# A four-layer graph network on one core: POOL starts a pair of indirect transfers when the even transfer two back has landed, instead of when the pair two back has, and each buffer has two semaphores, by the transfer's parity

## The chip, the core and the metric

The kernel runs on one core of one Trainium2 chip. The metric is the device time of one execution in microseconds (us), median of several runs. The engines are named as in the profile: PE (TensorE), DVE (VectorE), ACT (ScalarE), POOL (GpSimd), SP (SyncE).

## The reference, cut to what matters

A graph of 3125 nodes of 64 features and 103125 directed edges goes through four blocks; each block's output is added to x and x is normalised.

```python
edge_index = jnp.stack([src, dst])
x = _layernorm(x + _L0_gnn_ref(x, edge_index, ...))                 # 4 message layers
x = _layernorm(x + _L1_gnn_ref(x, edge_attr_64, edge_attr_9, ...))  # attention over edges
x = _layernorm(x + _L2_gnn_ref(x, edge_index, edge_attr_16, ...))   # one message layer
x = _layernorm(x + _L3_gnn_ref(x, edge_index))                      # normalised sum of neighbours
```

A message layer computes, for every edge, two dense layers with silu on the rows of its two end nodes, and sums the results per node:

```python
m = jnp.concatenate([hc[row], hc[col]], axis=1)
m = jax.nn.silu(m @ w1 + b1)
m = jax.nn.silu(m @ w2 + b2)
agg = jax.ops.segment_sum(m, row, num_segments=N) * C
```

## The kernel before

The kernel first sorts the edges by an end node (once by source, once by destination) into tiles of 128 edges, so that all edges of a tile have one of their ends in one block of 128 nodes. There are 832 tiles. The end in that block is fetched by a product with a one-hot matrix on PE. The other end can be any node, so its row is fetched from memory by an indirect transfer: one transfer, issued by POOL, brings one row for each of 128 partitions.

Five stages issue such transfers, all of them on POOL's one queue:

- The first scatter (line 917, function `scatter_s_pool`): 806 transfers of 8 bytes a row, to the sorted order by source. It runs beside the sorting by destination.
- The second scatter (line 935, `scatter_d_pool`): 806 transfers of 1136 bytes a row. A turn is four of them (EW = 4). PE and ACT compute the rows, ACT's copy `eo` (line 1082) ends them.
- The message layers (line 1193, `messages_pool` in `edge_messages`): four layers of block 0 and the one of block 2, 104 turns each, eight gathers a turn (W = 8) of 256 bytes a row, into one of four buffers `gx`. The gather of turn i waits for the copied indices `gi` (DVE, line 1278) and for a free buffer; DVE reads the rows three turns later, in the sum `pre_s` (line 1313).
- The logits of block 1 (line 1820, `logits_pool`): 208 turns, four gathers a turn (GT = 4) of 1280 bytes a row. The gather of turn i waits for the indices (DVE, line 1929) and for `gx_read`, with which DVE (line 1909) gives free the buffer of four turns back, right behind its product `kv` (line 1906). PE transposes the rows (line 1857) one turn later, after the first half of the turn's main products (line 1832) and before their second half. Its main products are of edges that are two turns older still.
- The last stage, block 3 (line 2415, `conv_pool`): 104 turns, eight gathers a turn of 256 bytes a row; PE multiplies them (line 2430) three turns later, DVE adds (line 2456).

Every stage runs as a software pipeline: `turns` unrolls the body four times (AHEAD = 4) inside a loop on each engine, and the engines meet only at semaphores. What matters here is how POOL throttles its own queue. Transfers go in pairs (PAIR = 2). Each pair has a semaphore, four of them a buffer in the message layers and the last stage (`rows_in[j][0..3]`), two in the logits and in the second scatter. Before the first transfer of a pair POOL waits until both transfers of the pair two back have landed. So when a pair starts, the pair just before it may still be under way. A landing adds 16 to the semaphore. An instruction that waits on POOL holds all that is behind it on POOL; POOL has nothing but these transfers in these stages.

The readers of a buffer (DVE line 1310, PE lines 1853 and 2425, DVE line 1928, ACT and DVE in `rows_gone`) wait for all its semaphores.

## Time and profile before

| what | value |
|---|---|
| median of 3 runs | 14786.38 us (14730.6 to 14797.07) |
| the profiled execution | 14804.43 us, its span on the core 14802.3 us |
| PE busy | 8646.8 us, 58% of the span |
| POOL busy | 7760.8 us, 52% |
| DVE busy | 5955.3 us, 40% |
| ACT busy | 2260.6 us, 15% |
| granted TensorE clock, mean | 0.77 |

The shares are means over stages that differ much, so that they bound nothing by themselves. The stages stand one behind another, and the time is the sum of their lengths; the first scatter alone runs beside other work.

### The profile page before, as it was taken

How to read it: one execution, taken by the hardware profiler on the slowest of the kernel's cores; microseconds unless marked ns; L12 is line 12 of the kernel's file. 1: busy time of each engine (PE TensorE's matmuls, PEld its weight loads, DVE VectorE, ACT ScalarE, POOL GpSimd, SP SyncE). 2: the span in 40 equal slices, each digit the busy share in tenths (PEclk: the TensorE clock that was granted, in tenths of full speed). 3: DMA queues.
4: the chain of work that ended last, by engine and by line, in shares of the span. 5: the costliest groups of instructions: out<-in, count | busy, mean ns of one | idle time of the engine just before them, and what ended most of it. 6: DMA issues, size and time to landing. Idle time of an engine off the chain costs nothing. (4 is left out here: it accounts for less than half of the span.)

```text
span 14802.3 us, 187298 instructions
## 1 busy us (share of the span) xinstructions
PE 8646.8 (58%) x45093; PEld 7115.8 (48%) x45094; DVE 5955.3 (40%) x14867; ACT 2260.6 (15%) x3991; POOL 7760.8 (52%) x7547
## 2 busy tenths in 40 slices
PE   2004778775555565555555555899994556664333
PEld 1004654444445455445444544788884545554232
DVE  5105730002333233333333333688888833333222
ACT  0000013330000100010001000355551000000000
POOL 5662025665555566546564656355552455554666
PEclk9999987876677666766676767899997867676555
DMA  1001333332111211121111111588884311111111
GB/s 24 1 1 61 108 121 119 117 111 54 38 38 36 62 39 39 37 60 39 38 39 48 39 37 39 169 250 251 251 251 110 103 42 41 41 41 29 22 22 22
DMA packets 853401, 1107.27 MB, mean 75 GB/s; under 512 B 336739, under 2 KB 530568, under 8 KB 852294
## 3 DMA queue, kind: packets, MB, share of 16 engines
q1 hardware_dynamic: 304698, 470.90, 10.9%
q0 software_dynamic: 264160, 418.34, 10.5%
q10 hardware_dynamic: 284332, 215.58, 5.6%
q8 instruction: 88, 1.44, 0.0%
q14 instruction: 123, 1.01, 0.0%
HBM read 896.28 MB, written 207.86 MB: 75 GB/s over the span
## 5 line engine op out<-in xcount | busy, mean ns | idle before, releaser
L1193 POOL DMA_INDIRECT gx_l<-xr,gi_l x4160 | 4231.1, 1017 | 3370.6 <-DVE gi_l L1278 2061.9
L1300 DVE TENSOR_TENSOR aggT_l<-aggT_l,psum 64x128 f32 x4160 | 1160.2, 279 | 3868.5 <-remote 1816.0
L1832 PE MATMUL psum<-cw,xa 128*128 128x256 f32 x6656 | 1519.2, 382 | 28.6 <-issue 21.3
L935 POOL DMA_INDIRECT slots_d<-eo,row_d x806 | 786.0, 975 | 1341.0 <-DVE eo L949 852.7
L1820 POOL DMA_INDIRECT gx<-xr,gi x832 | 896.0, 1077 | 1011.9 <-DVEq L1909 634.6
L1832 PEld LDWEIGHTS psum<-cw,xa 128*128 128x128 f32 x6656 | 1233.5, 190 | 252.9 <-issue 101.2
L1356 PE MATMUL psum<-ptab,oht 128*128 x6656 | 1017.9, 304 | 565.8 <-issue 506.4
L1356 PEld LDWEIGHTS psum<-ptab,oht 128*128 128x128 f32 x6656 | 953.8, 221 | 634.7 <-issue 633.7
L1232 PE MATMUL psum<-b,onesb 3*128 3x512 bf16 x520 | 260.7, 501 | 1650.6 <-ACT h_l L1259 1124.9
L2415 POOL DMA_INDIRECT gx_l<-xr,gi_l x832 | 834.6, 1003 | 473.9 <-DVE gi_l L2440 224.2
L1889 ACT COPY xT<-psum 32x512 f32<-32x512 f32 x1664 | 957.4, 575 | 611.8 <-remote 397.4
L917 POOL DMA_INDIRECT slots_s<-rec_s,row_s x806 | 801.7, 995 | 431.8 <-issue 418.5
L1234 PE MATMUL psum<-w,h_l 128*128 128x128 f32 x4160 | 879.4, 377 | 0.0
L1232 PEld LDWEIGHTS psum<-b,onesb 3*128 3x128 bf16 x520 | 49.5, 95 | 1720.1 <-issue 1691.8
L1234 PEld LDWEIGHTS psum<-w,h_l 128*128 128x128 f32 x4160 | 748.7, 270 | 181.3 <-issue 181.3
L1271 ACT ACTIVATE msg_l<-psum 128x512 f32<-128x512 f32 x520 | 310.6, 597 | 3315.7 <-remote 1843.7
L1259 ACT ACTIVATE h_l<-psum 128x512 f32<-128x512 f32 x520 | 310.6, 597 | 3296.6 <-remote 2372.8
L1245 PE MATMUL psum<-oh,msg_l 128*64 128x128 f32 x4160 | 733.6, 345 | 78.9 <-issue 78.4
L1313 DVE TENSOR_TENSOR pre_s_l<-psum,gx_l 128x512 f32<-128x512 f32 x520 | 359.7, 692 | 1008.3 <-remote 591.6
L1245 PEld LDWEIGHTS psum<-oh,msg_l 128*64 128x64 f32 x4160 | 644.1, 181 | 144.2 <-issue 132.5
L1245 PE MATMUL psum<-oh_b_l,msg_l 128*64 128x128 f32 x4160 | 678.2, 329 | 35.7 <-issue 30.1
L585 PE MATMUL psum<-oh_hi,oh_lo 128*128 128x25 bf16 x808 | 37.7, 183 | 1042.3 <-DVE oh_lo L522 692.0
(361 smaller groups left out, 13292.9 us busy)
## 6 DMA issues: line engine op xcount, KB each, us to landing
wkv<-slots_d ACTq DMA_DIRECT2D x208, 568.0 KB
kr<-keyrow_s SPq DMA_DIRECT2D x416, 256.0 KB
shb<-shT SPq DMA_DIRECT2D x1664, 64.0 KB
gx_l<-xr,gi_l POOLq DMA_INDIRECT x4992
vtab<-kv ACTq DMA_DIRECT2D x208, 256.0 KB
v_in<-vtab SPq DMA_DIRECT2D x104, 512.0 KB, 3.4
hT<-noderow SPq DMA_DIRECT2D x101, 512.0 KB
kr<-keyrow_d SPq DMA_DIRECT2D x208, 128.0 KB
```

Source lines behind the costliest of these rows:

```text
L917: scattered[j].at(pool.indirect_dma_start(slots["s"], bass.IndirectOffsetOnAxis(ap=row["s"][:, c:c + 1], axis=0), rec_s[:, c, :], None, bo ...
L935: e_gone[j][t // PAIR].at(pool.indirect_dma_start(slots["d"], bass.IndirectOffsetOnAxis(ap=row["d"][:, c0 + t:c0 + t + 1], axis=0), eo[j][ ...
L1193: pool.indirect_dma_start(gx[j][:, c_, :], None, xr, bass.IndirectOffsetOnAxis(ap=gi[j][:, c_:c_ + 1], axis=0)).then_inc(rows_in[j][h].sem ...
L1234: ins = pe.matmul(bank[2][:, q * P:(q + 1) * P], h1[:, q * P:(q + 1) * P], w2[:], start=False, stop=True, skip_group_check=True)
L1245: ins = pe.matmul(sums(j, t // per), msg[j][:, t * D:(t + 1) * D], ohs[j][:, t, :], start=t % per == 0, stop=(t + 1) % per == 0)
L1300: ins = dve.tensor_tensor(a, a, sums(j, h), ALU.add)
L1313: dve.tensor_tensor(pre_s[j][:], bank[0][:, :], gx[r][:, :, :].rearrange("p t f -> p (t f)"), ALU.add).then_inc(pre_done.sem, 1)
L1356: ins = pe.matmul(bank[0][:, t * D:(t + 1) * D], oht[:, t * P:(t + 1) * P], ptab[:, bass.ds(bl[t // PER["s"]] * D, D)], start=True, stop=True)
L1820: pool.indirect_dma_start(gx2[r][:, t, :], None, xr2, bass.IndirectOffsetOnAxis(ap=gi1[j][:, t:t + 1], axis=0)).then_inc(rows_in1[r][h].se ...
L1832: ins = pe.matmul(bank[2 + p][:, t % 2 * OKV:(t % 2 + 1) * OKV], xa[j][:, c, t * P:(t + 1) * P], cw[:, c, :], start=c == 0, stop=c == KC - 1)
L1889: ins = act.copy(xT2[j][q * DQ:(q + 1) * DQ, h, :], bank[0][h * DQ:(h + 1) * DQ, :])
L2415: pool.indirect_dma_start(gx[j][:, c_, :], None, xr, bass.IndirectOffsetOnAxis(ap=gi[j][:, c_:c_ + 1], axis=0)).then_inc(rows_in3[j][h].se ...
```

## The change

Transfers are no longer told apart by pairs but by parity (TURNS = 2). Each buffer, and each scatter, has two semaphores: one for its even transfers and one for its odd ones. POOL waits only ahead of an even transfer, until the even one two back has landed. The odd transfer behind it starts without a wait. Whether the odd transfer two or three back has landed is not asked. The number of waits on POOL is the same, one for two transfers; the readers of a buffer wait for two semaphores where they waited for four (logits and second scatter: two before and after). Nothing that is computed or moved changes.

```diff
-PAIR = 2
+TURNS = 2
...
             for c in range(EC):
-                j = c // PAIR % 3
+                j = c % TURNS
...
-                if c >= 2 * PAIR and c % PAIR == 0:
-                    two_back = scattered[(c // PAIR - 2) % 3]
-                    pool.wait_ge(two_back.sem, two_back.n)
+                if c >= TURNS and c % TURNS == 0:
+                    pool.wait_ge(scattered[j].sem, scattered[j].n)
...
                 for t in range(i * EW - c0, EW):
-                    if i and t % PAIR == 0:
-                        two_back = e_gone[(i - 1) % AHEAD][t // PAIR]
+                    if (i or t >= TURNS) and t % TURNS == 0:
+                        two_back = e_gone[j if t >= TURNS else (i - 1) % AHEAD][t % TURNS]
...
                         for c_ in range(W):
-                            h = c_ // PAIR
-                            if c_ % PAIR == 0 and (h >= 2 or k.has(0, 1)):
-                                s_, two_back = (0, rows_in[j][h - 2]) if h >= 2 else (1, rows_in[k.buf(1, AHEAD)][h + 2])
-                                pool.wait_ge(two_back.sem, two_back.n + k.uses(s_, AHEAD) * (16 * PAIR))
+                            h = c_ % TURNS
+                            if c_ >= TURNS and h == 0:
+                                pool.wait_ge(rows_in[j][h].sem, rows_in[j][h].n + (k.uses(0, AHEAD) - 1) * (16 * W // TURNS) + 16 * (c_ // TURNS))
+                                pool.nop(nofuse=True)
+                            elif c_ < TURNS and k.has(0, 1) and h == 0:
+                                of = rows_in[k.buf(1, AHEAD)][h]
+                                pool.wait_ge(of.sem, of.n + k.uses(1, AHEAD) * (16 * W // TURNS))
                                 pool.nop(nofuse=True)
...
                     for t in range(GT):
-                        h = t // PAIR
-                        if t % PAIR == 0 and k.has(0, 1):
-                            two_back = rows_in1[k.buf(1, AHEAD)][h]
-                            pool.wait_ge(two_back.sem, two_back.n + k.uses(1, AHEAD) * (16 * PAIR))
+                        h = t % TURNS
+                        if t >= TURNS and h == 0:
+                            pool.wait_ge(rows_in1[r][h].sem, rows_in1[r][h].n + (k.uses(0, AHEAD) - 1) * (16 * GT // TURNS) + 16 * (t // TURNS))
+                            pool.nop(nofuse=True)
+                        elif t < TURNS and k.has(0, 1) and h == 0:
+                            of = rows_in1[k.buf(1, AHEAD)][h]
+                            pool.wait_ge(of.sem, of.n + k.uses(1, AHEAD) * (16 * GT // TURNS))
                             pool.nop(nofuse=True)
```

The last stage has the same edit as the message layers, and the readers' loops over `range(W // PAIR)` become loops over `range(TURNS)`.

On POOL, one turn inside the loop of the first message layer stands like this before. The names in brackets are the semaphores that a row waits for; `s_rows_in1_2` is buffer 1, pair 2.

```order
L1183 REGISTER_ALU
L1185 REGISTER_ALU [waits s_gi_set]
L1193 DMA gx2_l0<-xr,gi2_l0 128x64 [waits s_pre_done,s_rows_in1_2]
L1193 DMA gx2_l0<-xr,gi2_l0 128x64
L1193 DMA gx2_l0<-xr,gi2_l0 128x64 [waits s_rows_in1_3]
L1193 DMA gx2_l0<-xr,gi2_l0 128x64
L1193 DMA gx2_l0<-xr,gi2_l0 128x64 [waits s_rows_in2_0]
L1193 DMA gx2_l0<-xr,gi2_l0 128x64
L1193 DMA gx2_l0<-xr,gi2_l0 128x64 [waits s_rows_in2_1]
L1193 DMA gx2_l0<-xr,gi2_l0 128x64
```

After the change the same turn is:

```order
L1182 REGISTER_ALU
L1184 REGISTER_ALU [waits s_gi_set]
L1195 DMA gx2_l0<-xr,gi2_l0 128x64 [waits s_pre_done,s_rows_in1_0]
L1195 DMA gx2_l0<-xr,gi2_l0 128x64
L1195 DMA gx2_l0<-xr,gi2_l0 128x64 [waits s_rows_in2_0]
L1195 DMA gx2_l0<-xr,gi2_l0 128x64
L1195 DMA gx2_l0<-xr,gi2_l0 128x64 [waits s_rows_in2_0]
L1195 DMA gx2_l0<-xr,gi2_l0 128x64
L1195 DMA gx2_l0<-xr,gi2_l0 128x64 [waits s_rows_in2_0]
L1195 DMA gx2_l0<-xr,gi2_l0 128x64
```

The transfers stand in the same order. The third row waits for the pair 4 and 5 of the turn before and becomes a wait for transfer 6 of that turn, and the later ones wait for transfers 0, 2 and 4 of the same turn.

On POOL, one turn of the logits loop before:

```order
L1788 REGISTER_ALU
L1788 REGISTER_ALU [waits s_gi1_set]
L1820 DMA gx22<-xr2,gi10 128x320 [waits s_turned1,s_gx_read,s_rows_in1_0]
L1820 DMA gx22<-xr2,gi10 128x320
L1820 DMA gx22<-xr2,gi10 128x320 [waits s_rows_in1_1]
L1820 DMA gx22<-xr2,gi10 128x320
```

And after:

```order
L1790 REGISTER_ALU
L1790 REGISTER_ALU [waits s_gi1_set]
L1825 DMA gx22<-xr2,gi10 128x320 [waits s_turned1,s_gx_read,s_rows_in1_0]
L1825 DMA gx22<-xr2,gi10 128x320
L1825 DMA gx22<-xr2,gi10 128x320 [waits s_rows_in2_0]
L1825 DMA gx22<-xr2,gi10 128x320
```

The wait ahead of the third transfer was for the second pair of the turn before (`s_rows_in1_1`); it is now for the first transfer of the same turn (`s_rows_in2_0`).

## Rows read from the trace of the kernel before

**Rows 1.** The view by windows: busy us (x instructions) of each engine, granted TensorE clock, DMA share, GB/s.

```profile
81.00:1235.00 1154.00, 102.69 (x811) 58.08 (x811) 220.78 (x281) 0.00 (x0) 801.43 (x806) 1.00 0.04 6
...
2066.00:3362.00 1296.00, 1021.44 (x3197) 530.16 (x3195) 59.82 (x247) 433.17 (x598) 785.73 (x806) 0.79 0.35 116
...
4858.00:6272.00 1414.00, 800.74 (x4539) 686.25 (x4537) 473.90 (x1179) 127.95 (x216) 840.35 (x832) 0.69 0.19 45
...
9389.00:11171.00 1782.00, 1739.42 (x9031) 1505.84 (x9032) 1531.64 (x3076) 995.99 (x1858) 896.04 (x832) 0.99 0.84 250
...
11882.00:13461.00 1579.00, 964.40 (x5494) 853.05 (x5494) 475.72 (x1187) 147.36 (x301) 852.64 (x831) 0.70 0.18 41
...
13546.00:14771.00 1225.00, 374.01 (x1642) 357.84 (x1642) 311.62 (x1016) 0.00 (x0) 834.58 (x832) 0.50 0.12 22
```

**Rows 2.** The page's costliest groups: indirect transfers that POOL issues, in four stages.

```profile
L1193 POOL DMA_INDIRECT gx_l<-xr,gi_l x4160 | 4231.1, 1017 | 3370.6 <-DVE gi_l L1278 2061.9
...
L935 POOL DMA_INDIRECT slots_d<-eo,row_d x806 | 786.0, 975 | 1341.0 <-DVE eo L949 852.7
...
L1820 POOL DMA_INDIRECT gx<-xr,gi x832 | 896.0, 1077 | 1011.9 <-DVEq L1909 634.6
...
L2415 POOL DMA_INDIRECT gx_l<-xr,gi_l x832 | 834.6, 1003 | 473.9 <-DVE gi_l L2440 224.2
```

**Rows 3.** POOL in order of time, layer stage: start us, us, in brackets idle before and releaser.

```profile
3383.55 0.94 POOL L1193 DMA_INDIRECT gx_l<-xr,gi_l  x1 [0.30 <-issue]
...
3386.05 0.94 POOL L1193 DMA_INDIRECT gx_l<-xr,gi_l  x1 [0.31 <-DMA gx_l<-xr,gi_l]
```

**Rows 4.** POOL in order of time, layer stage, two turns and the next start.

```profile
6023.57 1.72 POOL L1193 DMA_INDIRECT gx_l<-xr,gi_l  x1 [9.22 <-DVE gi_l L1278]
...
6043.34 0.94 POOL L1193 DMA_INDIRECT gx_l<-xr,gi_l  x1 [0.30 <-issue]
...
6049.67 1.72 POOL L1193 DMA_INDIRECT gx_l<-xr,gi_l  x1 [5.38 <-DVE gi_l L1278]
```

**Rows 5.** All engines in order of time, logits stage, one turn.

```profile
10005.91 0.94 POOL L1820 DMA_INDIRECT gx<-xr,gi  x1 [3.46 <-DVEq L1909]
...
10005.92 0.34 ACTq L1877 DMA_DIRECT2D wkv<-slots_d  x1
...
10007.50 0.60 PE L1857 MATMUL psum<-ident,gx 128*64 128x128 f32 x4
...
10010.00 1.30 POOL L1820 DMA_INDIRECT gx<-xr,gi  x1 [0.30 <-issue]
...
10012.82 0.69 DVE L1906 TENSOR_TENSOR kv<-gx,wkv 128x512 f32<-128x512 f32 x1
...
10014.46 0.94 POOL L1820 DMA_INDIRECT gx<-xr,gi  x1 [3.16 <-DVEq L1909]
```

**Rows 6.** POOL in order of time, logits stage, where a transfer ended the wait.

```profile
10024.30 0.95 POOL L1820 DMA_INDIRECT gx<-xr,gi  x1 [0.30 <-issue]
...
10031.81 0.94 POOL L1820 DMA_INDIRECT gx<-xr,gi  x1 [3.49 <-DMA gx<-xr,gi]
```

**Rows 7.** POOL in order of time, last stage, four turns.

```profile
13968.50 1.14 POOL L2415 DMA_INDIRECT gx_l<-xr,gi_l  x1 [4.42 <-DVE gi_l L2440]
...
14009.79 0.94 POOL L2415 DMA_INDIRECT gx_l<-xr,gi_l  x1 [0.30 <-issue]
...
14015.87 1.13 POOL L2415 DMA_INDIRECT gx_l<-xr,gi_l  x1 [5.13 <-DVE gi_l L2440]
```

**Rows 8.** POOL in order of time, second scatter.

```profile
2513.69 0.97 POOL L935 DMA_INDIRECT slots_d<-eo,row_d  x1 [0.30 <-issue]
...
2516.29 1.01 POOL L935 DMA_INDIRECT slots_d<-eo,row_d  x1 [0.30 <-DMA slots_d<-eo,row_d]
```

**Rows 9.** Waits of DVE over the run: us in total, times, longest.

```profile
DVE aggT_l L1300 <- issue: 1348.0, 1461, 18.7
```

**Rows 10.** DVE in order of time, last stage.

```profile
14109.98 0.22 DVE L2456 TENSOR_TENSOR conv<-conv,psum 128x64 f32 x1 [3.25 <-issue]
```

More of the change, by code:

```diff
@@ L891, in first_column @@
             return min(i * EW, EC - EW)
-        scattered = [sig(f"scattered{j}") for j in range(3)]
+        scattered = [sig(f"scattered{j}") for j in range(TURNS)]
         feats_in = [sig(f"feats_in{j}") for j in range(2)]
@@ L896, in build @@
         rec_in = sig("rec_in")
-        e_gone = [[sig(f"e_gone{j}_{h}") for h in range(EW // PAIR)] for j in range(AHEAD)]
+        e_gone = [[sig(f"e_gone{j}_{h}") for h in range(TURNS)] for j in range(AHEAD)]
         def group_dmas(g):
@@ L939, in rows_gone @@
         def rows_gone(eng, i):
-            for h in range(EW // PAIR):
-                eng.wait_ge(e_gone[i % AHEAD][h].sem, 16 * PAIR * (i // AHEAD + 1))
+            for h in range(TURNS):
+                eng.wait_ge(e_gone[i % AHEAD][h].sem, 16 * (EW // TURNS) * (i // AHEAD + 1))
         def records_dve(i):
@@ L982, in table_s_sp @@
         def table_s_sp():
-            for j in range(3):
+            for j in range(TURNS):
                 sp.wait_ge(scattered[j].sem, scattered[j].n)
@@ L1156, in edge_messages @@
             keys_in = [sig(f"keys_in{j}") for j in range(2)]
-            rows_in = [[sig(f"rows_in{j}_{h}") for h in range(W // PAIR)] for j in range(AHEAD)]
+            rows_in = [[sig(f"rows_in{j}_{h}") for h in range(TURNS)] for j in range(AHEAD)]
             feat_in = [sig(f"feat_in{j}") for j in range(2)]
@@ L1308, in turn @@
                         dve.wait_ge(local_done.sem, local_done.n + i + 1)
-                        for h in range(W // PAIR):
-                            dve.wait_ge(rows_in[r][h].sem, rows_in[r][h].n + k.uses(3, AHEAD) * (16 * PAIR))
+                        for h in range(TURNS):
+                            dve.wait_ge(rows_in[r][h].sem, rows_in[r][h].n + k.uses(3, AHEAD) * (16 * W // TURNS))
                         if k.has(3, 2):
@@ L1336, in edge_messages @@
             for j in range(AHEAD):
-                for h in range(W // PAIR):
-                    rows_in[j][h].n += 16 * PAIR * len(range(j, n, AHEAD))
+                for h in range(TURNS):
+                    rows_in[j][h].n += 16 * W // TURNS * len(range(j, n, AHEAD))
             for j in range(2):
@@ L1605, in scatters_end @@
             for j in range(AHEAD):
-                for h in range(EW // PAIR):
+                for h in range(TURNS):
                     sp.wait_ge(e_gone[j][h].sem, e_gone[j][h].n)
@@ L1778, in build @@
         keys_in1 = [sig(f"keys_in{j}") for j in range(2)]
-        rows_in1 = [[sig(f"rows_in{j}_{h}") for h in range(GT // PAIR)] for j in range(AHEAD)]
+        rows_in1 = [[sig(f"rows_in{j}_{h}") for h in range(TURNS)] for j in range(AHEAD)]
         wrows_in = [sig(f"wrows_in{j}") for j in range(2)]
@@ L1851, in turn @@
                     i, j, r = k.i(1), k.buf(1), k.buf(1, AHEAD)
-                    for h in range(GT // PAIR):
-                        pe.wait_ge(rows_in1[r][h].sem, rows_in1[r][h].n + k.uses(1, AHEAD) * (16 * PAIR))
+                    for h in range(TURNS):
+                        pe.wait_ge(rows_in1[r][h].sem, rows_in1[r][h].n + k.uses(1, AHEAD) * (16 * GT // TURNS))
                     upto(pe, "xT_set", k, 1, 1)
@@ L1926, in turn @@
                         r = k.buf(2, AHEAD)
-                        for h in range(GT // PAIR):
-                            dve.wait_ge(rows_in1[r][h].sem, rows_in1[r][h].n + k.uses(2, AHEAD) * (16 * PAIR))
+                        for h in range(TURNS):
+                            dve.wait_ge(rows_in1[r][h].sem, rows_in1[r][h].n + k.uses(2, AHEAD) * (16 * GT // TURNS))
                     dve.tensor_copy(gi1[j][:], gidx["d"][:, bass.ds(i * GT, GT)]).then_inc(s1["gi1_set"].sem, 1)
@@ L1965, in build @@
         for j in range(AHEAD):
-            for h in range(GT // PAIR):
-                rows_in1[j][h].n += 16 * PAIR * (G // AHEAD)
+            for h in range(TURNS):
+                rows_in1[j][h].n += 16 * GT // TURNS * (G // AHEAD)
         for j in range(2):
@@ L2398, in build @@
         tile_added = sig("part_added")
-        rows_in3 = [[sig(f"rows_in{j}_{h}") for h in range(W // PAIR)] for j in range(AHEAD)]
+        rows_in3 = [[sig(f"rows_in{j}_{h}") for h in range(TURNS)] for j in range(AHEAD)]
         def conv_pool():
@@ L2423, in turn @@
                     pe.wait_ge(oh_set.sem, oh_set.n + i + 1)
-                    for h in range(W // PAIR):
-                        pe.wait_ge(rows_in3[j][h].sem, rows_in3[j][h].n + k.uses(3, AHEAD) * (16 * PAIR))
+                    for h in range(TURNS):
+                        pe.wait_ge(rows_in3[j][h].sem, rows_in3[j][h].n + k.uses(3, AHEAD) * (16 * W // TURNS))
                     if k.has(3, 2):
@@ L2470, in build @@
         for j in range(AHEAD):
-            for h in range(W // PAIR):
-                rows_in3[j][h].n += 16 * PAIR * len(range(j, n3, AHEAD))
+            for h in range(TURNS):
+                rows_in3[j][h].n += 16 * W // TURNS * len(range(j, n3, AHEAD))
         join()
```

13 lines of the change are left out of this document (8 added, 5 removed).

## The prediction

> **What bounds the kernel now.** I read the view by windows first, one window for each stage with indirect transfers [rows 1], and look for the engine without slack. Then the page's groups [rows 2] for what POOL waits for, and last the order in time inside each stage [rows 3 to 8].
>
> The first scatter (81 to 1235 us) has PE and DVE nearly idle and POOL at 801 of 1154 us, but the sorting goes on for 800 us behind it, until the second scatter starts at 2066. It is beside the path. In the second scatter PE is busy 1021 of 1296 us; a turn of four transfers takes 1296 / 202 = 6.4 us. In the message layers nobody is full: PE 801, POOL 840 of 1414 us. A turn is 1414 / 104 = 13.6 us, and 1579 / 104 = 15.2 us in the layer of block 2. In the logits PE is busy 1739 of 1782 us and DVE 1532: a turn is 1782 / 208 = 8.57 us. In the last stage POOL is busy 835 of 1225 us and PE 374; a turn is 11.8 us.
>
> "Busy" leaves out the 0.30 us that POOL sits between two transfers, so POOL's own pace has to be put together: 0.945 + 0.30 = 1.25 us a transfer, 2.50 us a pair, 10.0 us a turn of eight. Two turns of the layers run from 6023.57 to 6043.34 + 0.94, 20.7 us for 16 transfers, then POOL waits 5.4 us for DVE's indices, and the period is 26.1 us [rows 4]. In the last stage four turns run from 13968.50 to 14010.73, 42.2 us, in a period of 47.4 us [rows 7]. So POOL has 5 us free in 26 and in 47. Its waits are for DVE: the indices of line 1278, or `gx_read` of line 1909 [rows 2]. POOL is nowhere the bound, and nearly so in the last stage.
>
> **The new wait and its price.** The number of waits stays. What changes is how far back each looks. Now a pair waits for transfers that began 5.0 and 3.75 us before it at the pace of 1.25 us; after, for one that began 2.50 us before it. It costs nothing if that one has landed by then, and POOL has reacted.
>
> How long a landing takes: the transfer that starts at 3383.55 is the last of the pair that is waited for just ahead of 3386.05, where the releaser is a transfer and the idle time no longer than usual. It landed between 3385.74 and 3386.05, so 2.2 to 2.5 us after its start [rows 3]. In the second scatter the same reading of 2513.69 and 2516.29 gives 2.3 to 2.6 us [rows 8]. How long POOL needs from a release to the start: `kv` of line 1906 ends at 10013.51, `gx_read` follows, and the transfer starts at 10014.46, 0.95 us later [rows 5]; this has other steps in it. The least is the ordinary gap of 0.30 us. Between the ends I take 0.65. A pair then takes 2.35 + 0.65 = 3.0 us instead of 2.50 with 256-byte rows, with bounds of 2.50 (2.2 + 0.30, nothing lost) and 3.45 (2.5 + 0.95). For the 1136-byte rows I take 3.15 (2.6 to 3.55). The odd transfer is issued without a wait, behind it nothing is late.
>
> **Message layers.** Four pairs: 12.0 us. The transfers are a bit longer than 0.945 us in the mean, 1.017 [rows 2], which adds 8 x 0.07 = 0.6: 12.6 us a turn against 13.6. In the two turns of [rows 4], 8 pairs x 0.5 = 4.0 us come out of an idle time of 5.4 us. A gather has three turns until it is read, so that a late POOL is not felt in the next turn. Cover is left, but thin; for shorter turns among the 416 I charge 0.1 us each: **+40 us**. Without cover (3.45 us a pair: 14.4 us a turn) it would be +0.8 x 416 = +330. The layer of block 2 has 2.6 us a turn to spare: 0.
>
> **Last stage.** Four turns are 16 pairs. 48.0 us, and of the 2.5 us by which today's run exceeds 32 x 1.25 - 0.30 I keep half: 49.2 against 47.4. It is the one stage where POOL becomes the bound outright: 1.8 x 26 = **+50 us** (0 to +220 at 3.45 us a pair).
>
> **Second scatter.** A turn of two pairs takes 6.3 us against 6.4 today. POOL can no longer make up for a wait for ACT's `eo`, which it does now at 5.1 us a turn. I charge 0.2 us x 202 = **+40 us** (0 to +140 at 3.55 us a pair). **First scatter:** even 0.9 us a pair more on 403 pairs is 360 us, under the 830 us that POOL then has until the second: 0.
>
> **Logits.** Here a landing takes much longer. Transfers 0 and 1 of a turn start at the same moment as the wide loads `wkv` (10005.91 and 10005.92) [rows 5], and the DMA engines are busy 0.84 [rows 1]. Where a transfer ended POOL's wait, it started 7.51 us after the second one of the pair waited for [rows 6], so this landed some 6.6 us after its start. At 10014.46 the same wait was already over when `gx_read` came, so transfer 1 had landed by 10013.5, 6.35 us after its start at about 7.16. For transfer 0 I take 5.9 us.
>
> Today transfers 0 to 3 start within 4.1 us (10005.91 to 10010.00), and transfer 3 can be 4 us on its way without harm. After, transfer 2 starts at 5.9 + 0.65 = 6.55 us after transfer 0, transfer 3 1.4 us later, and lands, with the wide loads done, in 3.3 us (2.4 to 4.5): 11.25 us after transfer 0. With the 0.95 from `gx_read` to transfer 0, a gather is there 12.2 us after its buffer was freed, 3 us later than now. The loop that this lies on: PE transposes the gather (10007.50), does the second half of its main products, DVE adds and frees a buffer at 10013.51, 6.0 us; the gather into it 12.2 us; 0.5 us to the next but one turn's transposes. That is two turns: 18.7 / 2 = 9.35 us against 8.57, 0.78 x 208 = **+160 us**. With 2.4 us for the last landing and 5.0 for transfer 0 it is 8.45, nothing; with 6.6 and 4.5 it is 10.3, +360 us.
>
> PE runs in order, so while it waits for the rows ahead of line 1857, the second half of the main products behind it waits too; that is why this stage has no cover.
>
> The readers' fewer semaphores save one sequencer step a turn, on engines that wait anyway: 0.
>
> **Sum.** 40 + 50 + 40 + 160 = 290 us. The profiled execution took 14804 us, 18 over the median shown. 15094 in its terms, **15080 us** in those of the median, 2.0% more.
>
> **What a page says against it.** The Trainium skill, "DMA: Bandwidth & Descriptors", section "Anatomy of one DMA — SWDGE (gpsimd) path", gives a transfer about 2.0 us plus its bytes at 436 GB/s. For the gathers of 32 KB that is an estimate of 2.1 us, near the 2.2 to 2.5 read above; for the 164 KB of the logits it would be 2.4 us, and the logits would lose nothing; the trace shows 6.6 us there.
>
> **Rivals.**
>
> - *The message layers join in.* While POOL issues without a break, DVE has long gaps without a releaser: 1348 us in all ahead of line 1300 [rows 9], and in the last stage 3.25 us ahead of a single addition [rows 10]. If such slow spells last as long as POOL's run of transfers does, each pair's 0.5 us lengthens the turn in full: 4 x 0.5 x 520 turns = 1040 us, in place of 40: about 16080. It decides from where the period follows POOL's run. Against it: POOL's idle time closes the gap between run and period, in the other engines' rhythm. Values between, near 15400, come out if a third of it does. 17%.
> - *The logits keep their pace.* If transfer 0 lands in 5.0 us or less and transfer 3 in 2.4, the loop of two turns fits (8.45 us). With the bound of 2.50 us a pair elsewhere and something for the second scatter, +0 to +60: 14830. For it: transfers 2 and 3 are no longer in the way of 0 and 1. Against it: [rows 6]. The page's rule above comes out here. 15%.
> - *Faster.* The slow spells of DVE come while POOL has up to four transfers under way; after, never more than three. If this halves the 1348 us of [rows 9], 674 us are won against the 290 lost: about 14400. It decides from a share of 290 / 1348, two tenths. For it: the gaps have no other releaser. Against it: POOL's pace, not their count, may be the cause, and that slows by a sixth only. 11%.
> - *The change doesn't bite*, because everything has landed within 2.50 us in every stage, is the lower bound of the second rival.
>
> **How the numbers follow.** The forecast, POOL's waits felt in the logits, the last stage and the second scatter, has 57%; and a range of its own of 14880 to 15400: the terms' bounds add up to 0 and to 1050 us, and hardly stand all at one end together. 10% lie above 15600, 10% below 14780. So the range is 14780 to 15600. A measurement of this kernel tells about 0.5% (74 us) from no change. Faster by more: 11%; within it: 14%; slower by more: 75%.
>
> **What the profile after would show.** Right: POOL's idle time in the four stages on the path is released by its own transfers, a pair takes 2.9 to 3.1 us in the layers and the last stage; the logits take 9.2 to 9.6 us a turn, with PE idle ahead of line 1857 and its busy share near 0.9; the layers stay at 1400 to 1430 us. Wrong: a layer above 1450 us (first rival), logits under 1800 us (second), fewer gaps without a releaser at line 1300 (third). The sum would also fail if PE's clock, 0.99 in the logits [rows 1], fell to its lower level with the new idle time; in the layers, where PE is idle half the time, it is granted 0.69.

## The result and the profile after

The changed kernel takes 14282.9 us (median of 4 runs, 14281.47 to 14289.83) beside 14786.05 us for the kernel before: ratio 0.9668, 95% interval 0.9644 to 0.9692. It is 3.3% faster, where 2% slower was predicted. The profiled execution took 14289.8 us, 515 less than that of the kernel before.

The view by windows, one window for each stage as in [rows 1] (busy us and count of PE, PEld, DVE, ACT, POOL; granted clock, DMA share, GB/s), of the changed kernel:

```profile
81.00:1450.00 1369.00, 695.71 (x3752) 588.33 (x3752) 802.19 (x2693) 55.19 (x131) 803.50 (x806) 0.64 0.23 69
1450.00:2858.00 1408.00, 1131.33 (x3149) 582.66 (x3149) 87.10 (x247) 414.91 (x591) 787.83 (x807) 0.74 0.32 107
...
4278.00:5642.00 1364.00, 1034.35 (x4699) 897.56 (x4697) 483.03 (x1217) 131.84 (x224) 803.23 (x832) 0.63 0.19 47
...
8584.00:10783.00 2199.00, 1851.26 (x9040) 1601.28 (x9041) 1533.64 (x3080) 997.12 (x1860) 874.44 (x832) 0.93 0.69 203
11495.00:12869.00 1374.00, 1004.34 (x5661) 890.25 (x5661) 483.68 (x1217) 151.93 (x311) 799.28 (x832) 0.74 0.20 48
12928.00:14258.00 1330.00, 375.54 (x1648) 359.18 (x1648) 314.89 (x1028) 0.00 (x0) 797.64 (x832) 0.50 0.11 21
```

Read the first row against [rows 1]: in the same stretch, beside the first scatter, DVE now executes 2693 instructions where it executed 281, and PE 3752 where it executed 811. That is the sorting by destination. The first scatter itself got longer (1154 to 1369 us), but the second one starts at 1450 us, not at 2066. The table gives the length of each stage, from these windows and those of the kernel before:

| stage | before, us | after, us | difference | predicted |
|---|---|---|---|---|
| start of the second scatter | 2066 | 1450 | -616 | 0 |
| second scatter | 1296 | 1408 | +112 | +40 |
| four message layers | 5656 | 5435 | -221 | +40 |
| layer of block 2 | 1579 | 1374 | -205 | 0 |
| logits | 1782 | 2199 | +417 | +160 |
| last stage | 1225 | 1330 | +105 | +50 |
| between the stages | | | -107 | 0 |
| sum | | | -515 | +290 |

The last row but one is what is left, the time between stages, such as 4778 to 4858 us before and 4227 to 4278 after. So three of the four predicted losses came, each two to three times larger, and under them lies a gain of 1150 us that the sum did not have.

Where the waits went shows in the groups of waits (us in total, times, longest), first of the kernel before, two rows that the prediction did not look at:

```profile
DVE aggT_l L1300 <- remote: 1816.0, 166, 29.0
...
DVE oh_hi L520 <- remote: 884.0, 67, 21.0
```

then of the changed kernel:

```profile
DVE pre_s_l L1315 <- DMA gx_l<-xr,gi_l: 3684.5, 520, 25.9
...
POOL gx_l L1195 <- DMA gx_l<-xr,gi_l: 1371.2, 1256, 9.7
...
POOL gx L1825 <- DMA gx<-xr,gi: 948.5, 356, 5.6
...
DVE aggT_l L1302 <- issue: 250.2, 1259, 0.6
...
DVE oh_hi L520 <- PE psum L585: 68.3, 54, 2.2
```

"remote" is the profile's word for a release that it can match to no instruction or transfer nearby; only one core is in use. Before, DVE's additions into `aggT_l` waited 1816 us for such releases and 1348 us for nothing that is seen [rows 9]; the sort's `oh_hi` waited 884 us. After, "remote" is gone ahead of `aggT_l` and down to 15.8 us in 6 waits ahead of `oh_hi`, "issue" ahead of `aggT_l` is down to 250 us with a longest of 0.6 us in place of 18.7, and what DVE waits for in the layers is the gathers, 520 times in 520 turns. POOL has become the bound in the layers.

The views leave out the short steps in which an engine's sequencer computes with registers between its instructions; the trace files hold them. In the kernel before, such a step of DVE takes 0.05 us in the median, but 514 of 17120 took 0.5 us or more, most of them near 0.7. In the layer of [rows 1] the first of them comes 7.0 us after the start of one of POOL's runs of transfers, none sooner. In the changed kernel DVE has none among 17074.

### The profile page after: what moved, and what is told of

It reads as the page before. It is cut to its first block and busy times, and to the rows that moved or that the text cites. A ratio compares the mean times of both kernels' runs of the same rounds, so it can differ in the third digit from the quotient of the medians.

```text
span 14288.0 us, 187007 instructions
## 1 busy us (share of the span) xinstructions
PE 9801.4 (69%) x45093; PEld 8103.8 (57%) x45094; DVE 5953.6 (42%) x14867; ACT 2244.2 (16%) x3991; POOL 7497.5 (52%) x7547
## 5 line engine op out<-in xcount | busy, mean ns | idle before, releaser
L1195 POOL DMA_INDIRECT gx_l<-xr,gi_l x4160 | 4023.5, 967 | 3088.5 <-issue 1406.2
L1358 PE MATMUL psum<-ptab,oht 128*128 x6656 | 1464.8, 411 | 387.8 <-issue 338.1
L1358 PEld LDWEIGHTS psum<-ptab,oht 128*128 128x128 f32 x6656 | 1388.7, 317 | 509.9 <-issue 509.9
L1837 PEld LDWEIGHTS psum<-cw,xa 128*128 128x128 f32 x6656 | 1319.9, 202 | 232.7 <-issue 42.9
L1208 PE MATMUL psum<-ident,pre_s_l 128*128 128x128 f32 x2080 | 403.7, 327 | 1132.2 <-DVE pre_s_l L1315 1131.9
L2423 POOL DMA_INDIRECT gx_l<-xr,gi_l x832 | 797.6, 959 | 591.5 <-DMA gx_l<-xr,gi_l 399.2
L1236 PE MATMUL psum<-w,h_l 128*128 128x128 f32 x4160 | 1033.7, 427 | 0.0
L1236 PEld LDWEIGHTS psum<-w,h_l 128*128 128x128 f32 x4160 | 885.6, 314 | 216.5 <-issue 216.5
L1208 PEld LDWEIGHTS psum<-ident,pre_s_l 128*128 128x128 f32 x2080 | 264.0, 163 | 1260.7 <-issue 1260.7
L1247 PE MATMUL psum<-oh_b_l,msg_l 128*64 128x128 f32 x4160 | 818.7, 379 | 1.0 <-DVE oh_b_l L1291 1.0
L1247 PEld LDWEIGHTS psum<-oh_b_l,msg_l 128*64 128x64 f32 x4160 | 745.5, 204 | 57.5 <-issue 56.4
```

What stands on the lines that cost most here:

```text
L1195: pool.indirect_dma_start(gx[j][:, c_, :], None, xr, bass.IndirectOffsetOnAxis(ap=gi[j][:, c_:c_ + 1], axis=0)).then_inc(rows_in[j][h].sem ...
L1208: ins = pe.transpose(bank[1][:, q * P:(q + 1) * P], pre_s[j][:, q * P:(q + 1) * P], ident[:])
L1236: ins = pe.matmul(bank[2][:, q * P:(q + 1) * P], h1[:, q * P:(q + 1) * P], w2[:], start=False, stop=True, skip_group_check=True)
L1247: ins = pe.matmul(sums(j, t // per), msg[j][:, t * D:(t + 1) * D], ohs[j][:, t, :], start=t % per == 0, stop=(t + 1) % per == 0)
L1358: ins = pe.matmul(bank[0][:, t * D:(t + 1) * D], oht[:, t * P:(t + 1) * P], ptab[:, bass.ds(bl[t // PER["s"]] * D, D)], start=True, stop=True)
L1837: ins = pe.matmul(bank[2 + p][:, t % 2 * OKV:(t % 2 + 1) * OKV], xa[j][:, c, t * P:(t + 1) * P], cw[:, c, :], start=c == 0, stop=c == KC - 1)
```

## The experiments

The kernels of one set ran on one chip beside shared runs of the kernel before. That kernel did not take the same time in all sets, though its runs within a set agree within 0.7%. Each ratio below is to the runs of its own set.

| set | kernel before, us | kernels (us, ratio, 95% interval) |
|---|---|---|
| first | 14786 | changed 14283, 0.9668 |
| 1 | **11660** | e2 11894, 1.0200 (1.0183 to 1.0217); e4 13288, 1.1391 (1.1372 to 1.1410) |
| 2 | 14474 | e5 14480; e6 14267, 0.9843 (0.9825 to 0.9861); e7 14583, 1.0061 (1.0041 to 1.0081); e8 14461, 0.9994 (0.9976 to 1.0013) |
| 3 | **11661** | e9 12494, 1.0712 (1.0694 to 1.0730); e10 11907, 1.0207 (1.0190 to 1.0224); e11 13298, 1.1405 (1.1386 to 1.1424); e12 12960, 1.1112 (1.1094 to 1.1131) |
| 4 | 14456 | e13 14438; e14 14259, 0.9862 (0.9832 to 0.9892); e15 13611, 0.9413 (0.9386 to 0.9440); e16 13955, 0.9660 (0.9629 to 0.9691) |
| 5 | 14747 | e17 13513, 0.9164 (0.9149 to 0.9179); e18 14136, 0.9576 (0.9557 to 0.9595); e19 13695, 0.9284 (0.9266 to 0.9302); e20 14287, 0.9686 (0.9670 to 0.9703) |

I call 11660 us the lower level and 14456 to 14786 us the upper level. The level is not tied to one chip: sets 1 and 2 carry the same chip number on record and were at different levels. It shows in every trace of any kernel: in the fourteen traces at the upper level SP has 34 to 214 register steps of 0.5 us or more, in the six at the lower level neither SP nor DVE nor POOL has one. PE and ACT have none at either. What sets the level is open. No trace was taken of the kernel before at the lower level; its stages there are read from e2.

**The rule in the first scatter alone (e2, e10, e18).**

```diff
-                j = c // PAIR % 3
+                j = c % TURNS
...
-                if c >= 2 * PAIR and c % PAIR == 0:
-                    two_back = scattered[(c // PAIR - 2) % 3]
-                    pool.wait_ge(two_back.sem, two_back.n)
+                if c >= TURNS and c % TURNS == 0:
+                    pool.wait_ge(scattered[j].sem, scattered[j].n)
```

> The kernel before, with the changed rule in the first scatter alone. Theory A: the first scatter takes 1368 us in place of 1153, yet the second begins near 1450 us in place of 2066, because sorting by destination, on the other engines, is no longer held up; the rest is as before: 14786 - 616 = about 14170 us. Rival (the 616 us are of the later stages' making, or the sort was bound by something else): 14786 + 0 to 215 us.

> The changed rule in the first scatter alone, as run before. Where the kernel before takes about 14500 us or more beside it: the second scatter starts near 1447 us in place of 2054, so 14474 - 607 = 13870 us. Where it takes 11660 us: 11894 us again.

> The changed rule in the first scatter alone. Where the kernel before takes 14440 us or more: second scatter from 1447 us instead of 2050, all later stages as before: 13840 to 13880 us. Rival (the sort's delay is made up or moved elsewhere): 14300 us or more. Where it takes 11660 us: 11900 us again.

e2 met the lower level, which no theory had foreseen. Its windows show the first scatter with the changed rule, then the stages with the old rule there (second scatter, a layer, logits, block 2's layer, last stage):

```profile
81.00:1445.80 1364.80, 693.88 (x3752) 587.57 (x3752) 795.81 (x2693) 55.15 (x131) 803.39 (x806) 0.88 0.23 69
1445.90:2520.00 1074.10, 906.50 (x3149) 482.57 (x3149) 62.16 (x247) 416.28 (x591) 788.34 (x806) 0.89 0.42 141
...
4830.00:5926.00 1096.00, 831.21 (x4687) 724.41 (x4686) 484.95 (x1217) 131.56 (x224) 808.15 (x832) 0.75 0.24 59
7174.00:8933.00 1759.00, 1725.84 (x9027) 1506.11 (x9028) 1531.39 (x3077) 995.57 (x1857) 897.78 (x832) 0.99 0.86 253
9649.00:10724.00 1075.00, 877.38 (x5659) 777.31 (x5659) 487.67 (x1221) 151.23 (x310) 810.90 (x832) 0.83 0.25 62
10783.00:11864.00 1081.00, 375.56 (x1648) 359.19 (x1648) 316.06 (x1032) 0.00 (x0) 819.67 (x832) 0.50 0.13 25
```

Against [rows 1] a layer takes 1096 us in place of 1414, block 2's 1075 in place of 1579, the last stage 1081 in place of 1225, by the same code: 1096 / 832 = 1.32 us a transfer, POOL's own pace of 1.25 and a little. The logits alone are unchanged. The waits in the same trace:

```profile
DVE aggT_l L1300 <- issue: 59.6, 90, 3.2
```

and none for "remote". At the lower level the changed rule in the first scatter only costs its own 2% (11894 and 11907 us, e2 and e10). In set 5, at the upper level, the same kernel is 4.2% faster; its windows there:

```profile
81.00:1445.30 1364.30, 695.52 (x3752) 588.35 (x3752) 803.20 (x2693) 55.08 (x131) 801.14 (x806) 0.64 0.23 69
1445.40:2750.50 1305.10, 1022.15 (x3149) 529.91 (x3149) 61.76 (x247) 427.66 (x591) 785.53 (x806) 0.78 0.34 116
2763.00:4153.00 1390.00, 776.60 (x4481) 668.07 (x4482) 476.14 (x1184) 118.70 (x199) 844.57 (x832) 0.69 0.18 42
```

The second scatter starts at 1445 us, as in the changed kernel, and later stages are as slow as in [rows 1]. 14747 - 14136 = 611 us, the 616 of the table; the time itself is above the 13840 to 13880 expected, which were worked out from the quicker kernel before of other sets. The first scatter's rule alone makes that term.

**The rule in the first scatter and the layers (e4, e11, e19).** The edits of the change at the lines of `scatter_s_pool` and `edge_messages`, the rest as before.

> The changed rule in the first scatter and the message layers, the rule of before in the second scatter, the logits and the last stage. From the stages of the two traces, if they add: 14283 - 417 (logits) - 111 (second scatter) - 105 (last stage) = about 13650 us. Under theory A the second scatter and the last stage keep their slow steps but not their slower transfers. If the stages don't add (the gain in one is owed to the rule in another), 14000 to 14283 us.

> The changed rule in the first scatter and the message layers, as run before. Where the kernel before takes about 14500 us or more beside it: the changed kernel's 14267 less 412 (logits), 99 (second scatter) and 120 (last stage) = 13636 us. Where it takes 11660 us: 13288 us again.

> The changed rule in the first scatter and the message layers alone. Where the kernel before takes 14440 us or more: 14260 - 415 - 115 - 116 = about 13610 us. Where it takes 11660 us: 13290 us again.

At the upper level 13695 us: the changed kernel's 14287 of the same set less 592, where 417 + 112 + 105 = 634 were expected. The gain and the losses of the stages nearly add. At the lower level it is 14% slower than the kernel before. Its layer there:

```profile
2537.00:3891.00 1354.00, 1032.12 (x4635) 895.34 (x4635) 481.35 (x1216) 122.99 (x206) 803.42 (x832) 0.63 0.19 43
```

At the upper level a layer under the changed rule takes as long (1364 us above). With the changed rule the layers take one time, with the old rule two.

**Both kernels again (e5, e6, e13, e14, e20).** No edit.

> The kernel before, unchanged, for its trace. In the run of the kernel with the changed rule in the first scatter alone, the kernel before took 11660 us beside it, not 14786. Theory D (the kernel before has two regimes, and in the one of the first measurement POOL's transfers without a break hold up the other engines): where it takes about 11660 us, the message layers run at 1.30 us per transfer (1.69 before), the sort by destination is done when the first scatter is, and DVE shows no sequencer steps near 0.7 us. Where it takes about 14786 us, all is as in [rows 1].

> The changed kernel, unchanged. Theory D: its own time hardly depends on the regime, since POOL waits for landings anyway: 14200 to 14300 us; where the kernel before takes about 11660 us beside it, the ratio is near 1.22, slower. Rival (whatever made the kernel before faster by 21% makes the changed one faster too): 11100 to 11600 us.

> The kernel before, unchanged, for its trace in whichever regime this batch shows. At about 11660 us: message layers at 1.30 us per transfer, the second scatter begins at the first one's end near 1235 us, and the slow sequencer steps of DVE in the message layers are gone. At 14470 us or more: as in the earlier trace, second scatter from about 2055 us, message layers at 1.63 to 1.70 us.

> The changed kernel, unchanged. Theory D: 14240 to 14300 us in either regime, as its stages waited for landings in both kernels' traces so far. Beside 11660 us for the kernel before that is a ratio of 1.22 to 1.23; beside 14474 us, 0.985. Rival: in the regime of 11660 us it is also quicker, 11500 to 13500 us.

> The changed kernel, unchanged. 14250 to 14300 us in either regime, with the ratio 1.22 to 1.23 beside 11660 us and 0.985 beside 14470 us (theory D); a rival is that it too falls to 11500 to 13500 us where the kernel before does.

All three sets were at the upper level, so the changed kernel has no run beside 11660 us. Its time is steady (14259, 14267, 14287), while the kernel before moves from 14438 to 14786 within that level, and the ratio from 0.967 to 0.986 with it. In two of these sets the gain is under 2%, though clear of the runs' spread. What moves is the layers: the four of block 0 take 5656 us in the first trace of the kernel before and 5428 in e13, but 5435 and 5418 in those of the changed kernel (first, e14). The second scatter's start doesn't move: 2066 and 2049 us before, 1450 and 1446 after. So the sort is the steady part of the gain. The kernel before at 14438 us (e13) has the waits of the first trace:

```profile
DVE aggT_l L1300 <- remote: 1365.3, 147, 37.3
DVE aggT_l L1300 <- issue: 1335.2, 1614, 15.2
...
DVE oh_hi L520 <- remote: 731.8, 62, 20.9
```

**The wait further back (e7).** Semaphores by the transfer's number modulo four in place of two, and at an even transfer a wait for the even one four back.

```diff
-TURNS = 2
+TURNS = 4
...
-                            if c_ >= TURNS and h == 0:
+                            if c_ >= TURNS and h % 2 == 0:
```

> The changed kernel with four semaphores per buffer in place of two, and the wait before an even transfer for the even one four back in place of two back. Theory D and theory A: the time is that of the kernel before beside it, within 1% (about 11660 us in the one regime, 14786 in the other), since only the wait's distance counts. Theory B (the number and grouping of the semaphores): it stays at the changed kernel's 14283 us or near it.

14583 beside 14474: the kernel before's time and 0.6%, with its waits ("remote" 1446.0 us, "issue" 1403.1 ahead of `aggT_l`). That the semaphores are told apart by the transfer's number and not by pair gains nothing. The reach of the wait is what counts.

**Empty instructions (e8), memsets (e9, e15).** The waits of before, and ahead of every pair in the first scatter, the layers and the last stage either twelve empty instructions or eight memsets of one column each:

```diff
+                            if c_ % PAIR == 0:
+                                for _ in range(12):
+                                    pool.nop(nofuse=True)
```

```diff
+            for x in range(8):
+                ins = pool.memset(pad[:, slot * 8 + x:slot * 8 + x + 1], 0.0)
```

> The kernel before with twelve empty instructions of POOL ahead of every pair in the first scatter, the message layers and the last stage. In the regime of 14786 us: theory A says faster, 13700 to 14100; theory C says no gain. In the regime of 11660 us POOL is the bound, and the pause can only cost: 2900 pairs by 0.3 to 1 us, 12500 to 14500 us.

> The kernel before with eight one-column memsets of POOL (128x1 each) ahead of every pair in the first scatter, the message layers and the last stage, which hold POOL's datapath up, as the twelve empty instructions did not; waits and semaphores of before. They compute nothing that is used. Where the kernel before takes about 14500 us or more beside it: a break theory says DVE's slow steps and the late start of the second scatter go, faster by 300 to 1200 us; a theory of depth (transfers under way) says no gain. Where the kernel before takes about 11660 us: POOL is the bound, and the time rises by 2900 pairs times the pause that the trace shows.

> Eight one-column memsets ahead of every pair, as run before (12494 us beside 11660). Where the kernel before takes 14470 us or more: if a break of 0.16 to 0.3 us per pair is enough to let the other engines through, the time is near 12500 to 13900 us; if depth counts or the break is too short, 14400 to 14900 us.

The empty instructions cost nothing and gain nothing: in the trace of e8 the transfers still start 1.25 us apart. So they left POOL's stream as it was, and e8 is no test of a break. The memsets do hold it up. POOL in order of time in e15 (start us, us):

```profile
4002.67 0.31 POOL L912 MEMSET pad<- 128x1 f32 x8
4003.13 0.95 POOL L1211 DMA_INDIRECT gx_l<-xr,gi_l  x1
4004.38 0.95 POOL L1211 DMA_INDIRECT gx_l<-xr,gi_l  x1 [0.30 <-issue]
4005.32 0.32 POOL L912 MEMSET pad<- 128x1 f32 x8
4005.79 0.95 POOL L1211 DMA_INDIRECT gx_l<-xr,gi_l  x1 [0.15 <-issue]
```

In these rows a pair takes 2.66 us in place of 2.50, and POOL executes 23192 instructions more. At the upper level that makes the kernel 5.9% *faster*, by 845 us. Most of it, 530 us, is the sort: the second scatter begins at 1518 us in place of 2048 (e13), and `oh_hi`'s "remote" waits fall from 732 to 125 us. The layers gain less: the first takes 1289 us where it took 1346, `aggT_l` still has 978 us of "issue" and 1023 of "remote" (longest 16.2 us in place of 37.3), and ACT's "remote" waits ahead of `msg_l` rise from 1960 to 2425 us. DVE's long register steps are halved, 251 for 550. The last stage gains nothing (1222 us, 1211 before). At the lower level the same kernel is 7.1% slower. So work that computes nothing helps, in one level alone; no wait for a landing and no other number of transfers allowed under way is needed for it. The memsets break POOL's stream up and also slow it by 6%: e15 doesn't tell the two apart.

**One wait in four transfers (e12, e16).** Semaphores modulo four; in the first scatter, the layers and the last stage POOL waits for the even one two back at every second pair alone, and not at the others.

```diff
-                            if c_ >= TURNS and h == 0:
-                                pool.wait_ge(rows_in[j][h].sem, rows_in[j][h].n + (k.uses(0, AHEAD) - 1) * (16 * W // TURNS) + 16 * (c_ // TURNS))
+                            if c_ % 4 == 2:
+                                pool.wait_ge(rows_in[j][0].sem, rows_in[j][0].n + (k.uses(0, AHEAD) - 1) * (16 * W // TURNS) + 16 * (c_ // TURNS + 1))
```

> Four semaphores per buffer; in the first scatter, the message layers and the last stage POOL waits for the even transfer two back only ahead of every second pair (one break in four transfers, not two); second scatter and logits wait for the even one four back. Where the kernel before takes about 14500 us or more: a break theory says that a break each 5 us is enough, since before the slow steps begin 7 us after a run's start: message layers near 1.5 us per transfer, time 12500 to 13300 us; if only the rate counts, between far4 and the changed rule, 13600 to 14500 us. Where it takes 11660 us: half of the changed rule's cost in these stages, 12700 to 13000 us.

> One wait for a landing in four transfers, as run before (12960 us beside 11660). Where the kernel before takes 14470 us or more: break theory 12900 to 13400 us (POOL's own pace of 1.53 us is then the bound in the layers, and only the second scatter keeps its 230 us); if the pace alone counts, 13600 to 14500 us.

At the upper level (e16) the windows show the first scatter and a layer:

```profile
81.00:1232.50 1151.50, 106.09 (x883) 60.78 (x883) 234.53 (x299) 0.00 (x0) 801.96 (x806) 1.00 0.04 6
...
7361.00:8633.50 1272.50, 961.24 (x4699) 829.69 (x4697) 482.82 (x1221) 132.29 (x224) 857.88 (x832) 0.67 0.18 47
```

and at the lower level (e12) the first scatter and the same layer:

```profile
81.00:1402.00 1321.00, 695.71 (x3752) 588.40 (x3752) 795.03 (x2693) 55.18 (x131) 803.70 (x806) 0.51 0.24 71
...
6463.00:7736.00 1273.00, 992.28 (x4693) 856.80 (x4692) 482.21 (x1217) 131.47 (x224) 854.79 (x832) 0.65 0.18 47
```

The layer is the same at both levels, 1272.5 and 1273 us, and 90 us shorter than under the changed rule: a break of about 0.6 us once in 1272.5 / 208 = 6.1 us was enough there. DVE's long register steps are gone from this layer and from the last stage of e16. That fits the 7.0 us after which the first of them came in the kernel before: here POOL starts four transfers in about 5 us and pauses. It doesn't prove that the pause counts and not the pace, since POOL's own pace slows too, from 1.25 to 1.53 us a transfer (1272.5 / 832).

It was not enough in the first scatter: DVE executed 299 instructions beside it and the second scatter began at 2045 us, so the expected 12900 to 13400 us became 13955. POOL's wait for its own scatters hardly appears in that trace (15.1 us in 4 waits put down to DMA; in e12 261.9 us in 105). One might say that no break came about, because with the sort held up few other transfers run (6 GB/s in the window against 71) and the scatters land before the wait asks. But the trace has breaks there, such as the second row here (POOL, start us, us, idle before):

```profile
707.43 0.97 POOL L916 DMA_INDIRECT slots_s<-rec_s,row_s  x1 [0.30 <-issue]
709.52 0.97 POOL L916 DMA_INDIRECT slots_s<-rec_s,row_s  x1 [1.12 <-issue]
```

Of the 805 steps from one start to the next, 243 are over 1.6 us in e16 and 242 in e12; what differs is the steps over 2.5 us, 8 and 108. The whole stage takes no longer than under the old rule, 1151.5 us to 1154 in [rows 1]. Why these short breaks don't free the sort, while e15's still shorter ones do (its stage takes 1206.5 us), stays open.

**The parts together (e17).** The changed rule in the first scatter, one wait in four in the layers, the even one four back elsewhere.

> The changed rule in the first scatter, one wait in four transfers in the message layers, the waits of before (even transfer four back) in the second scatter, the logits and the last stage. Where the kernel before takes 14440 us or more: the kernel with one wait in four took 13955 us; less 600 us for a second scatter that begins near 1447 us instead of 2046, less 60 us in the last stage: about 13290 us. Where the kernel before takes 11660 us: that kernel took 12960 us; less 195 us in the last stage, plus about 45 us in the first scatter: 12810 us.

13513 us, 8.4% faster than the kernel before in its set (14747), 220 us over the 13290 expected. All of that may be the set: the kernel before took 291 us more there than in set 4, from whose kernels the 13290 was worked out. The layers under the same rule are slower too, 1292.5 us for the 1272.5 of e16, and DVE has long register steps in them again (27 in that layer). It is the fastest kernel at the upper level. At the lower level it wasn't run; there every kernel with a break was slower than the kernel before, by 2 to 14%.

## Why the prediction was wrong

**"It is beside the path."** The step that failed first, a term put at 0. The first scatter was given 830 us of cover, since the sorting went on behind it. I asked whether the longer scatter would be felt, and not why the sort was late. The answer stood in [rows 1], which show PE and DVE nearly idle beside the scatter: I read that as a property of the program, but the sort could run there and was held up: under the changed rule DVE executes 2693 instructions beside the scatter where it executed 281. With the rule in that stage alone the second scatter moves from 2066 to 1445 us and the time falls by 611 us (e18). That term is larger than the whole of the predicted +290.

**Message layers, "Cover is left, but thin".** I took the turn of 13.6 us as a rhythm of DVE's own, into which POOL's waits had to fit. It was not: the same program runs the turn in 1096 / 104 = 10.5 us in e2. Over the five layers e2 takes 1809 us less (5426 for 7235). What goes with the difference are DVE's gaps with no releaser and the late releases, 1348 and 1816 us at line 1300 alone, where e2 has 60 and none; their sum is above 1809 us, so not each of them cost time. After, POOL is the bound: four pairs of 3.28 us are 13.1 us a turn (1364 / 104). The price of a pair was taken as 3.0 us and bounded by 3.45, so it was a little low, but that is not what made the term wrong. The sign of the term was wrong, -426 us with block 2's layer in place of +40. In set 4 the four layers alone take 5428 us before (e13) and 5418 after (e14), near the +40; there the gain is in block 2's layer, -105 us. So how much the layers give depends on how slow the kernel before happens to be, and the sort's 600 us do not.

**The third rival had the direction, in part by luck.** "If this halves the 1348 us": it fell to 250, and the "remote" part, not in the rows I used, to nothing. Its 14400 us was 117 us off, but by two errors that nearly cancel: it set 674 us of gain against 290 of loss, and measured were 1150, half of them in the sort, which it didn't mention, against 634. Its reason was the number of transfers under way; e15 gains with that number left as it was. I had given it 11% because "POOL's pace, not their count, may be the cause". e15 bears out that the pace or its unbrokenness is a cause, and the change helps since it alters both.

**The first rival was right about the other level.** That POOL's longer pairs lengthen the layers' turn in full has the wrong sign here. At the lower level it is what the runs show: the five layers take 6812 us under the changed rule (e11) and 5426 under the old one (e2), 0.67 us a pair.

**Logits, +160.** Direction right, size wrong: +417, beyond the +360 of the bounds. The sum let transfer 2 wait for transfer 0's landing and left transfer 0 at 0.95 us behind `gx_read`. But transfer 0 of the next turn waits for this turn's transfer 2 by the same rule. POOL in order of time in the changed kernel:

```profile
9644.35 0.95 POOL L1825 DMA_INDIRECT gx<-xr,gi  x1 [3.40 <-DMA gx<-xr,gi]
...
9648.32 0.95 POOL L1825 DMA_INDIRECT gx<-xr,gi  x1 [1.35 <-DMA gx<-xr,gi]
...
9655.48 1.23 POOL L1825 DMA_INDIRECT gx<-xr,gi  x1 [4.82 <-DMA gx<-xr,gi]
...
9661.29 0.95 POOL L1825 DMA_INDIRECT gx<-xr,gi  x1 [3.31 <-DMA gx<-xr,gi]
...
9664.87 0.95 POOL L1825 DMA_INDIRECT gx<-xr,gi  x1 [1.39 <-DMA gx<-xr,gi]
```

Every pair here is released by a landing, and in the whole stage 356 of 416 are put down to one: 4.0, 7.2, 5.8 and 3.6 us, 10.3 us a turn here, 2199 / 208 = 10.6 in the mean. The trace files also record when POOL's wait ends. In this stage it ends 4.3 us in the median after the start of the transfer that is waited for (3.2 to 6.8 in nine tenths of the cases), and POOL starts the next one 0.70 us later. The 0.65 us put for POOL's reaction was nearly right; the landings' chain was missing. The loop that I costed ran through PE and DVE; the one that counts is POOL's own chain of landings. PE's busy share fell to 1851 / 2199 = 0.84 where near 0.9 was expected, and its granted clock fell too, from 0.99 to 0.93, named as a danger and not priced. The rule of the Trainium skill ("DMA: Bandwidth & Descriptors", "Anatomy of one DMA — SWDGE (gpsimd) path") gave 2.4 us for these landings. The trace doesn't agree: the median is 4.3 us, and even the short ones take 3.2.

**Second scatter and last stage.** A turn of the second scatter is 1408 / 202 = 7.0 us, 3.5 a pair where 3.15 was taken and 3.55 the bound; the last stage 1330 / 416 = 3.20 a pair where 3.0 was taken. Both inside the bounds and above the choice, and "POOL becomes the bound outright" was right for the last stage. In the last stage POOL's wait ends 2.47 us after the start waited for, and the next transfer starts 0.70 us after that; in the second scatter it is 2.54 and 0.79 us (medians from the trace files). Taken were 2.35 and 0.65, and 2.5 and 0.65. Both stages were also shorter without the disturbance (1074 and 1081 us in e2), so that their true cost is 334 and 249 us.

**The frame of the sum.** All terms were added to the time of one trace, as if its stages had only one length. At the lower level the changed kernel can be estimated from e11's 13298 us with the old rule's logits, second scatter and last stage (1763, 1074 and 1083 us) put at the changed ones (2199, 1408 and 1330): 14315 us, 23% over 11660. That level would have had the predicted sign, and far more than the predicted size. It is an estimate; no run shows it.

## What stays open

Why a set is at one level or the other. The same program differs, within a set nothing moves, and the chip number on record doesn't decide it. The changed kernel ran in all sets at the upper level and in neither at the lower one, but four and two sets are too few to tell that from chance. Which of POOL's doings holds the other engines up is open too, and whether it is the missing break or the pace. In the layers no run changes one without the other; in the first scatter e16 has more short breaks at the same length of the stage, and the sort stays held up. DVE's long register steps go with it in the layers, but not in the first scatter of the kernel before, where POOL has 233 of them and DVE none, though `oh_hi` waits. The Trainium skill ("SBUF — State Buffer", "Who interferes with whom") has a lock between DVE and POOL for whole instructions. The trace gives it no support as the cause: `aggT_l`'s addition takes 279 ns under the old rule at both levels (e13, e2) and 278 in the changed kernel, so DVE's work is not longer, it begins later. A late start alone would not exclude a lock; but SP, which only issues transfers here, has long register steps as well, and ACT's `msg_l` has "remote" waits, though ACT could be late through DVE and PE. In e13:

```profile
L1271 ACT ACTIVATE msg_l<-psum 128x512 f32<-128x512 f32 x520 | 311.2, 598 | 3458.2 <-remote 1960.0 <-PE psum L1234 1249.0 <-issue 249.1
```

## What to carry to other kernels

When an engine is idle and its wait names no releaser, ask whether it could run before calling the stage uncovered or covered: here a neighbour's stream of indirect transfers was what held it, and slowing that stream shortened the kernel. Price a throttle as a chain of its own, landing to landing, at every transfer that it applies to, turn boundaries included. And before adding terms to a stage's length, learn whether that length repeats in another set of runs, since even the same chip number gave both lengths in this case. The same change is worth -3.3% or (by the estimate) +23%. One wait in each pair, in four transfers or in none should be chosen stage by stage, by the level that the kernel will run at.

## What was not expected of the hardware

The kernel before has two times, 11660 us and 14456 to 14786 us, 24% to 27% apart, on the same program; a layer takes 1096 or 1346 to 1424 us. At the longer one, while POOL issues indirect transfers 1.25 us apart, single waits of DVE last up to 37 us without a releaser nearby ("remote", e13), ACT has such waits as well, and register steps of DVE that take 0.05 us in the median take about 0.7 us in 514 of 17120 cases, SP's in 209 of 6136. At the shorter one no such step was long, in six traces. Under the changed rule (a break of 0.5 to 0.8 us each pair) DVE's are gone at the longer one too, and SP's down to 38; with memsets that lengthen a pair by 0.16 us DVE has 251 left, and its waits at line 1300 go from 2701 to 2002 us. From the end of POOL's own wait to the start of the next transfer it took 0.70 us in the layers, the logits and the last stage of the changed kernel. Twelve empty instructions ahead of a pair took no time on POOL; eight one-column memsets took 0.31 us, of which 0.16 us lengthened the pair.
